# Graph kernel on one core: edge arrays loaded by two queues in pieces, gathers in another order, one wait on a store moved back

## What is computed

```
out_deg = segment_sum(ones, src); in_deg = segment_sum(ones, dst)
src_norm = clip(out_deg, 1) ** -0.5;  dst_norm = clip(in_deg, 1) ** -0.5
repeat 10 times:  f = f * src_norm;  agg = segment_sum(f[src], dst)
                  f = 0.9 * agg * dst_norm + 0.1 * feat
x = layernorm(x + f)                       # then three more layers
```

## Time and profile before

| | |
|---|---|
| median of 3 runs | 2887.84 us (2886.71 to 2887.98) |
| span of the profiled execution, first to last instruction | 2884.1 us |
| the profiled execution's own time beside its span | not recorded apart; the median of the runs is 3.7 us above the span |
| busy: DVE, POOL, ACT, PE | 2003.3, 1716.7, 621.6, 532.6 us |

### The profile page before, as it was taken

How to read it: one execution, slowest core, us unless ns; L and a number is a source line. 1 busy time by engine, 2 the same in 40 slices (tenths; PEclk the granted TensorE clock), 3 DMA queues, 4 the chain that set the end, 5 groups by cost and what they waited for, 6 DMA issues and landing times.

```text
span 2884.1 us, 24928 instructions
## 1 busy us (share of the span) xinstructions
PE 532.6 (18%) x3578; PEld 338.3 (12%) x3578; DVE 2003.3 (69%) x3750; ACT 621.6 (22%) x1382; POOL 1716.7 (60%) x1741
## 2 busy tenths in 40 slices
PE   4770000075000000000002022320245451000000
PEld 2330000074000000000002011220122220000000
DVE  6777888488945455545999577079778788667773
ACT  5982333032000000000012012441243330100000
POOL 5777777777047755645547776660346460717776
PEclk9995555598555555555556565555555555555555
DMA  6003332100012022221131201110000000100000
GB/s 209 21 12 96 97 99 85 24 14 13 1 59 33 10 27 20 24 21 59 60 62 23 63 11 9 56 49 16 5 6 7 6 8 37 30 5 9 9 9 9
DMA packets 100774, 101.69 MB, mean 35 GB/s; under 512 B 58048, under 2 KB 92528, under 8 KB 98808
## 3 DMA queue, kind: packets, MB, share of 16 engines
q1 hardware_dynamic: 47064, 80.35, 7.7%
q0 software_dynamic: 53664, 20.91, 7.5%
HBM read 38.06 MB, written 60.81 MB: 34 GB/s over the span
## 4 chain that ended last, share of the span: by engine, by line
DVE 32%; POOL 26%; issue 21%; DMA 8%; PE 5%; ACT 3%; DVEq 2%; SPq 1%; ACTq 1%; POOLq 0%
POOL SW L493 7%; POOL XS L493 7%; POOL cring L468 3%; POOL ring L772 3%; POOL out_dram L484 2%; DVE YW L1252 2%; DMA cring<-sums_by_list,cidx 2%; PE banks L2689 1%; POOL attention_by_edge L872 1%; POOL ring L865 1%; DVE RB L1252 1%; DVE SW L1380 1%; DVE SW L1372 1%; DVE SW L1392 1%; PE banks L2684 1%
## 5 line engine op out<-in xcount | busy, mean ns | idle before, releaser
L484 POOL DMA_INDIRECT out_dram<-ring,ridx x196 | 210.5, 1074 | 126.6 <-DVE ridx L2172 66.6
L493 POOL DMA_INDIRECT XS<-in_x_dram,xsi x196 | 197.5, 1008 | 81.6 <-issue 62.3
L493 POOL DMA_INDIRECT SW<-node_table,srci x196 | 200.3, 1022 | 62.8 <-issue 62.8
L891 POOL DMA_INDIRECT out_dram<-z4w,oidx x98 | 96.3, 982 | 223.6 <-ACT oidx L2443 193.9
L493 POOL DMA_INDIRECT XD<-in_x_dram,xdi x196 | 189.8, 968 | 62.6 <-issue 62.3
L468 POOL DMA_INDIRECT cring<-sums_by_list,cidx x128 | 123.7, 967 | 104.2 <-issue 76.5
L2558 PE MATMUL banks<-tl,dcar 128*128 128x32 f32 (+1 forms) x14 | 4.4, 404 | 781.8 <-DVEq L1362 595.6
L2476 PE MATMUL banks<-YW 128*128 128x392 f16 x784 | 139.5, 332 | 48.2 <-ACT YW L2253 38.6
L772 POOL DMA_INDIRECT ring<-x_by_edge,aidx x96 | 101.2, 1054 | 58.9 <-issue 28.6
L468 POOL DMA_INDIRECT cring<-sums_by_edge,cidx x56 | 52.9, 945 | 117.7 <-DVE cidx L1563 102.8
L994 DVE TENSOR_SCALAR YW<-YW,b_d 128x784 f16<-128x784 f16 x196 | 83.4, 425 | 48.3 <-PE banks L2476 46.4
(11 more groups left out here) (602 smaller groups left out, 3432.0 us busy)
## 6 DMA issues: line engine op xcount, KB each, us to landing
SW<-in_x_dram SPq DMA_DIRECT2D x20, 625.0 KB
out_dram<-SW SPq DMA_DIRECT2D x20, 625.0 KB
sums_by_list<-RB SPq DMA_DIRECT2D x2, 1800.0 KB
sums_by_edge<-RB SPq DMA_DIRECT2D x1, 3528.0 KB, 9.8
sums_by_list<-RB SPq DMA_DIRECT2D x2, 1600.0 KB
XS<-in_x_dram,xsi POOLq DMA_INDIRECT x196
list_values_by_edge<-RB SPq DMA_DIRECT2D x1, 3136.0 KB
attention_by_edge<-RB SPq DMA_DIRECT2D x1, 3136.0 KB
```

The source lines that it names most:

```text
L484: pool.indirect_dma_start(out=table, out_offset=off, in_=ring_row(h, j, w), in_offset=None, bounds_check=limit, oob_is_err=False).then_inc ...
L493: pool.indirect_dma_start(out=dest[:, t * w:(t + 1) * w], out_offset=None, in_=table, in_offset=bass.IndirectOffsetOnAxis(ap=idx[:, t:t + ...
L891: pool.indirect_dma_start(out=out[:, :], out_offset=bass.IndirectOffsetOnAxis(ap=oidx[:, b, t:t + 1], axis=0), in_=oring[b][:, t * D:(t + ...
```

## The change

- `src` and type are loaded by SP, `dst` and weight by ACT, each array as 112 rows, 15 rows and the last row. `src` and `dst` have the semaphore `s_in`, type and weight a new one, `s_in2`.
- DVE waits for `src` and `dst` only, makes `xsi` first and adds to `s_ids` at once. `ety16`, made from the types, moves behind the node table. The later counts of `s_ids` that ACT and PE wait for rise by one.
- POOL gathers 160 source columns, then (after the node table) 196 degree columns, then 36 source columns, then 148 target columns, later 38 and 10.
- The wait for the last node store and the two clears move behind the shift block; the second wait for the store at L1257 goes. The wait for `XS` moves ahead of `out_rows`, which overwrites `xsi`.

```diff
-        XD_EARLY, XD_MID = 136, 180
+        XS_AHEAD, XD_EARLY, XD_MID = 160, 148, 186
+        def load_edges(queue, a, tile, loaded):
+            rows = edges(a)
+            queue.dma_start(tile[0:P - 16, :], rows[0:P - 16, :]).then_inc(loaded, 16)
+            queue.dma_start(tile[P - 16:P - 1, :], rows[P - 16:P - 1, :]).then_inc(loaded, 16)
+            queue.dma_start(tile[P - 1:P, 0:LASTV], edges_last(a)).then_inc(loaded, 16)
...
-            for a, t in ((src, srci), (dst, dsti), (etype, etyi), (eweight, ew)):
-                sp.dma_start(t[0:P - 1, :], edges(a)).then_inc(s_in, 16)
-                sp.dma_start(t[P - 1:P, 0:LASTV], edges_last(a)).then_inc(s_in, 16)
+            load_edges(sp, src, srci, s_in)
+            load_edges(sp, etype, etyi, s_in2)
...
-            gather_edges(pool, x[:, :], xsi, XS, D, s_xs)
+            gather_edges(pool, x[:, :], xsi, XS, D, s_xs, range(0, XS_AHEAD))
             pool.wait_ge(s_ntw, 16 * HA_CH)
             gather_edges(pool, nt_d[:, :], srci, S, 4, s_ns)
+            gather_edges(pool, x[:, :], xsi, XS, D, s_xs, range(XS_AHEAD, T))
+            pool.wait_ge(s_ids, 2)
             gather_edges(pool, x[:, :], xdi, XD, D, s_xd, range(0, XD_EARLY))
...
-            dve.wait_ge(s_in, 16 * 8)
+            dve.wait_ge(s_in, 16 * 6)
+            st.seq(V.tensor_scalar(xsi[:, :], srci[:, :], float(N - 1), None, ALU.min))
+            dve.sem_inc(s_ids, 1)
...
-            dve.wait_ge(s_nout, 16 * CH)
-            st.do(V.memset(rhi[0], 0.0))
-            st.do(V.memset(rlo[0], 0.0))
...
             dve.wait_ge(s_ns, 16 * T)
-            dve.wait_ge(s_nout, 16 * CH)
             st.do(V.memset(rpos, 0.0))
...
                 st.seq(V.tensor_copy(part, lval.bitcast(I32)))
+            dve.wait_ge(s_nout, 16 * CH)
+            st.do(V.memset(rhi[0], 0.0))
+            st.do(V.memset(rlo[0], 0.0))
+            st.wait()
             dve.sem_inc(s_rc, 1)
...
+            dve.wait_ge(s_xs, 16 * T)
             out_rows(srcf, t1w[:, 0:T], osi)
-            dve.wait_ge(s_xs, 16 * T)
...
+            load_edges(act, dst, dsti, s_in)
+            load_edges(act, eweight, ew, s_in2)
             act.wait_ge(s_const, 13)
```

More of the change, by code:

```diff
@@ L325, in gnn_resnorm @@
         s_pad = sem("padding_set")
-        s_in = sem("edges_loaded")
+        s_in, s_in2 = sem("edges_loaded"), sem("types_and_weights_loaded")
         s_w = sem("weights_loaded")
@@ L958, in _ @@
             st.wait()
-            dve.wait_ge(s_in, 16 * 8)
+            dve.wait_ge(s_in, 16 * 6)
+            st.seq(V.tensor_scalar(xsi[:, :], srci[:, :], float(N - 1), None, ALU.min))
+            dve.sem_inc(s_ids, 1)
             st.do(V.tensor_scalar(srcf[:, :], srci[:, :], 0.0, None, ALU.add))
             st.do(V.tensor_scalar(dstf[:, :], dsti[:, :], 0.0, None, ALU.add))
-            st.do(V.tensor_scalar(ety16[:, :], etyi[:, :], 0.0, None, ALU.add))
-            st.do(V.tensor_scalar(xsi[:, :], srci[:, :], float(N - 1), None, ALU.min))
             st.do(V.tensor_scalar(xdi[:, :], dsti[:, :], float(N - 1), None, ALU.min))
@@ L1040, in _ @@
             dve.sem_inc(s_nt, 1)
+            dve.wait_ge(s_in2, 16 * 6)
+            st.do(V.tensor_scalar(ety16[:, :], etyi[:, :], 0.0, None, ALU.add))
             dve.wait_ge(s_w, 16 * (4 * 4 + 7))
@@ L2235, in take_roots @@
                 n_roots += count * len(kinds)
+            act.wait_ge(s_pad, 1)
+            load_edges(act, dst, dsti, s_in)
+            load_edges(act, eweight, ew, s_in2)
             act.wait_ge(s_const, 13)
-            act.wait_ge(s_ids, 2)
+            act.wait_ge(s_ids, 3)
             def high_digits(i, b, later=True):
@@ L2461, in _ @@
             tick = s_tick[3]
-            pe.wait_ge(s_ids, 3)
+            pe.wait_ge(s_ids, 4)
             for c in range(4):
```

## The result

The changed kernel takes 2836.6 us (median; 2832.41 to 2837.31), the kernel before 2887.91 us (2886.71 to 2888.37) beside it: ratio 0.9822, 95% interval 0.9808 to 0.9836. Predicted were 2835.2 us and a range of 2829 to 2843. The span went from 2884.1 to 2834.5 us, 49.6 less; 52.6 were predicted. The medians lie 2887.91 - 2836.6 = 51.3 us apart.

What follows compares the result with a forecast made beforehand. The late load, then POOL's gathers ending the meeting with DVE, were taken to bound the kernel. -10.8 - 37.9 + 1.1 - 5.0 = -52.6 took the span from 2884.1 to 2831.5; plus 3.7, 2835.2 us, range 2829 to 2843.

Steps and rivals of the forecast that it cites:

- The front, -10.8: Start of kernel: earlier load moves DVE's first index instruction from 22.30 to 11.5, and histogram through node pass by 10.8 us.
- Side by side on two of 16 engines: Load: even at the old rate, src and dst on two DMA engines would be there at 10.0, before DVE at 11.5.
- the upper bound of 14.8: Load: src and dst one after the other at 21 GB/s land at 14.8, 3.3 us behind DVE's arrival.
- The meeting, -37.9: DVE's wait for POOL's degrees before the shift block: degrees land before the node pass ends, saving 37.9 us beyond the front.
- The wait of 1.6 us for the node table: Before the degree gathers: POOL waits some 1.6 us for the node table's store and begins at 227.1.
- The room: End of node pass: the degrees are there 5.6 us before DVE needs them at 499.3.
- The wait for the store, +1.1: Behind the shift block: the moved store wait costs nothing; two clears come onto the path with a step's end, +1.1 us.
- The last piece, -5.0: Before the gather of sums_by_list: 10 target columns instead of 16 remove DVE's 5.03 us wait, -5.0 us.
- The late load: Rival at the start: DVE still waits for the load, costing 3.3 to 10.8 us, total 2838.5 to 2846; chance 0.10.
- late degrees: Rival after the node pass: degrees land after DVE is ready, up to 6 us, total 2835.2 to 2841; chance 0.09.
- an idle last piece: Rival at sums_by_list: the shorter last piece brings nothing, another equal wait standing behind it, total 2840.2; chance 0.07.
- the rival on the slower side: Histogram: PE at half clock, 1.2 us more on each of 49 groups, 57 us, total 2892; chance 0.02.

Runs made afterwards that it cites:

- the old load: Changed kernel with four whole arrays of 127 rows loaded by SP again, DVE waiting for all four: 2848.36 us, ratio 0.9868.
- one queue, pieces: Changed kernel with all four edge arrays loaded in pieces by SP alone, none by ACT: 2838.08 us, ratio 0.9832.
- the run with 176 columns: Changed kernel with 176 instead of 160 source columns gathered ahead of the degrees: 2852.86 us, ratio 0.9882.
- the run with the wait back: Changed kernel with the wait for the last node store and the two clears back behind the node pass: 2845.84 us, ratio 0.9861.
- the zeros on ACT: Changed kernel with DVE's opening 5.4 us memset of RB replaced by a copy of a zero column on ACT: 2828.87 us, ratio 0.9801.

## Why the prediction was right

**The front, -10.8.** Right: 22.30 - 11.53 = 10.8 at the first index instruction, 10.6 at the digits, POOL's first gather 11.5. The reason was half right. "Side by side on two of 16 engines" falls: whole arrays on two queues shared 22 GB/s and landed for DVE at 14.26, near the upper bound of 14.8. The cover before 11.5 came from the pieces. Missing from the sum were the 2.1 us of the histogram, which come from the instructions that the load's issues add on ACT and not from earlier edges.

**The meeting, -37.9.** Right: 50.2 less the 12.8 by which the node pass moved is 37.4, and the old load gave 37.4 as well. The wait of 1.6 us for the node table did not come: the histogram was shorter, and POOL was through with its 160 columns 1.1 us later than reckoned. With the histogram in its long form (one queue, pieces) there is a wait of 1.40 us, 0.30 of it the usual idle time between two gathers. The room was not 5.6 us but, by the run with 176 columns, about 3.4, since DVE came 2.0 us before the 499.3 of the prediction.

**The wait for the store, +1.1.** The mechanism is right, the wait costs nothing at its new place and 10.3 us at the old one. The term was too small: between the ranking's memset and the first rank step the lead shrank by 50.2 - 47.7 = 2.5 us. 1.2 is the clears; 1.3 is the gap of [2.99 <-issue] in the shift block, 1.68 before, in the run with the wait back and in the one with 176 columns. In all traces it is 1.68 or 1.69 us where DVE had waited for a DMA ahead of the block and 2.96 to 3.31 where it had not; why is not known.

**The last piece, -5.0.** Right: 4.7 in the trace, 4.5 undone.

**The sum** promised 3.0 us more than the span gave. The histogram gave 2.1 that were not foreseen. Against it stand 1.4 by which the stretch with the clears cost more than its +1.1; 0.5, 0.3 and 0.2 at the meeting, the last piece and the digits; and 2.6 us that the lead lost between the first rank step (47.7) and the payload's gather (45.1). As far as the runs show, that last loss is no cost of the change. The same stretch took 373.2 us in the trace of before and 375.7 in that of the changed kernel, but 373.3 with the old load and 373.4 with the zeros on ACT, which have the changed order too; over all thirteen traces it lies between 373.2 and 375.8. Single executions differ by that much there, and the two that are compared lie near the two ends. From what within the stretch the difference comes stays open.

That the median fell nearer than the span, 1.4 us away, was luck. The prediction added 3.7 to the span, from before. In every run on record with both numbers the time stands only 1.7 to 1.8 above its own span, so the traced execution of before was some 2 us faster than the median beside it; with the changed kernel the median stood 2.1 above.

POOL's room before the first list gather was 33.42 us, not 40: 148 columns took 1.334 us each, not 1.30, and began 1.5 us later.

**The rivals.** The late load did not come, nor late degrees, nor an idle last piece. PE had its high clock in the histogram, a granted clock of 1.00 from 14 to 205 us, as in the earlier trace rows, so the rival on the slower side fell too.

## What to carry to other kernels

When two engines meet in one wait, read both chains: the load was worth 7.1 us while POOL's chain ended the meeting and 11.8 once it did not (some 2 us of it from the faster histogram). After a wait is gone, look at what its engine does right ahead of it: a 5.4 us memset stood in front of the index instruction, and moving it to the idle ACT brought the ranking another 5.6 us forward, where the whole new load had brought 12.8. Split a load by what spreads it over the DMA engines before giving it another queue. And before a loss of 2 us between two traces is explained, compare the same stretch in other traces of the same code.

## What the runs showed of the hardware that was not expected

- Two queues, each with an array of 127 rows, moved 22 GB/s together at a share of 0.07, as one did; pieces of 112 and 15 rows reached 0.77 and 192 GB/s on two queues, 0.41 and 99 GB/s on one. The Trainium skill ("DMA: Bandwidth & Descriptors", "Why a DMA increments its semaphore by 16 and not by 1") gives 127 rows one engine; the trace agrees, with its share of 0.07.
- A memset of 128 x 6400 on POOL held an integer `TENSOR_SCALAR` of DVE for 4.87 us in place of 0.26, but not a DVE memset (0.27 us); inside a write of the same size by ACT an integer `TENSOR_SCALAR` took 0.25.
- Seven fulfilled waits ahead of a loop on ACT shortened a 200 us histogram by 2.16 us: an idle time of 0.21 us ahead of every second long instruction shrank to that of the others, about 0.12.
- DVE's idle time ahead of `wcol` was 2.99 us where it had not waited for a DMA before the shift block, 1.68 us where it had.
